# Gated scan: the second half of the causal convolution on VectorE instead of in TensorE's in-projection

## The reference, cut to what matters

```
xz = x @ W_in                          # 128 -> 512
xc, z = split(xz, 2)                   # 256 channels each
xt = causal depthwise conv of xc, 4 taps, own taps for each channel
u  = silu(xt)
dt_raw, B_raw = split(u @ W_x, 2)      # 16 + 16
dt = clip(softplus(dt_raw @ W_dt + b_dt), 1e-4, 1)
ub = u * (B_raw @ W_Bp)
h[t] = h[t-1] * (1 - dt[t]) + ub[t]
out = ((h + D_param * u) * silu(z)) @ W_out
```

## Time and profile before

| what | value |
|---|---|
| median of three runs | 3280.31 us |
| the profiled execution | 3282.22 us |
| its span | 3279.4 us |
| TensorE, busy share of the span | 79%, mean granted clock 0.91 |
| VectorE, busy share | 68% |
| ScalarE, busy share | 48% |
| GpSimd, busy share | 62% |

### The profile page before, as it was taken

The page is one execution under the profiler, slowest core; times in us unless marked ns, Lnnn a source line. Parts: engine busy times, 40 slices in busy tenths (PEclk is TensorE's granted clock), DMA queues, the critical chain, the costliest instruction groups (busy, mean ns, idle before and its releaser), DMA issues. The chain is left out here.

```text
span 3279.4 us, 43901 instructions
## 1 busy us (share of the span) xinstructions
PE 2580.4 (79%) x12400; PEld 1850.5 (56%) x12400; DVE 2222.7 (68%) x3998; ACT 1575.7 (48%) x2668; POOL 2018.0 (62%) x1643
## 2 busy tenths in 40 slices
PE   5799994996689999348996678788877875579782
PEld 4599993443579999327995233333332322559672
DVE  5656663786766666683332699999999998653333
ACT  4433333884533333333333667567577662443330
POOL 0377771232057776305772789999999784335776
PEclk9999997998599999569998899999999999589997
DMA  6111112100411111422332689889888886312333
GB/s 180 32 48 48 46 48 56 39 26 1 135 37 48 46 47 40 134 72 61 87 87 43 243 291 310 278 296 305 285 291 301 288 300 207 103 40 76 92 90 85
DMA packets 287326, 429.78 MB, mean 131 GB/s; under 512 B 59196, under 2 KB 196799, under 8 KB 287200
## 3 DMA queue, kind: packets, MB, share of 16 engines
q1 hardware_dynamic: 251744, 357.54, 33.1%
q0 software_dynamic: 35456, 70.86, 9.3%
HBM read 367.71 MB, written 62.39 MB: 131 GB/s over the span
## 5 line engine op out<-in xcount | busy, mean ns | idle before, releaser
L683 POOL DMA_INDIRECT m_rows<-rows_in,m_source x568 | 554.0, 975 | 588.6 <-SPq L580 222.2
L1593 PE MATMUL s_y_ps<-s_prod,ident 128*128 128x512 f32 x1024 | 522.0, 634 | 214.3 <-DVE s_prod L1880 214.3
L1558 POOL TENSOR_TENSOR s_dBu<-s_du,s_B_row 128x1024 f32<-128x1024 f32 x256 | 602.4, 2359 | 84.6 <-DVE s_dA L1873 71.1
L1873 DVE TENSOR_TENSOR_SCAN s_dA<-s_dA,s_dBu 128x1024 f32<-128x1024 f32 x256 | 585.6, 2287 | 44.3 <-POOL s_dBu L1558 44.3
L721 PE MATMUL m_A_ps<-m_rowsT,m_own 128*128 128x256 f32 x2272 | 569.0, 383 | 2.1 <-ACT m_rowsT L763 1.1
L737 PE MATMUL m_Y_ps<-m_own,m_hid 128*128 128x128 f32 x4544 | 556.1, 276 | 3.6 <-issue 3.6
L737 PEld LDWEIGHTS m_Y_ps<-m_own,m_hid 128*128 128x128 f32 x4544 | 531.4, 192 | 5.7 <-issue 5.6
L1593 PEld LDWEIGHTS s_y_ps<-s_prod,ident 128*128 128x128 f32 x1024 | 180.9, 195 | 523.3 <-DVE s_prod L1880 325.9
L773 ACT ACTIVATE m_act_a<-m_A_ps,m_own 128x256 f32<-128x256 f32 x568 | 238.5, 471 | 434.7 <-PE m_A_ps L721 318.9
L721 PEld LDWEIGHTS m_A_ps<-m_rowsT,m_own 128*128 128x128 f32 x2272 | 414.9, 193 | 48.8 <-ACT m_rowsT L763 1.9
L1694 ACT ACTIVATE s_dA<-s_delta,s_decay 128x1024 f32<-128x1024 f32 x256 | 286.0, 1118 | 311.0 <-DVE s_prod L1880 306.2
(11 more groups left out here) (241 smaller groups left out, 3543.9 us busy)
## 6 DMA issues: line engine op xcount, KB each, us to landing
s_B_row<-s_bc_rows SPq DMA_DIRECT2D x256, 512.0 KB, 5.7
s_C_row<-s_bc_rows SPq DMA_DIRECT2D x256, 512.0 KB, 6.0
rows_out<-m_y_sb SPq DMA_DIRECT2D x142, 128.0 KB
rows_in<-m_xs SPq DMA_DIRECT2D x64, 256.0 KB, 2.3
m_rows<-rows_in,m_source POOLq DMA_INDIRECT x568
s_got<-rows_by_token SPq DMA_DIRECT2D x16, 512.0 KB, 5.0
m_got<-rows_by_token SPq DMA_DIRECT2D x32, 256.0 KB, 3.9
rows_by_token<-m_y_sb,m_target POOLq DMA_INDIRECT x284
```

Source lines behind the costliest of these rows:

```text
L683: pool.indirect_dma_start(rows[:, b % AHEAD, r, :], None, c.rows_in, bass.IndirectOffsetOnAxis(source[:, 2 * b + r:2 * b + r + 1], 0)).the ...
L1558: nc.gpsimd.tensor_tensor(dBu[q % RING][:, :], du[s % 2][:, h, :], B_row[q % RING][:, :], ALU.mult).then_inc(dBu_ready, 1)
L1593: ins = nc.tensor.matmul(y_ps[:, at(cc, 512)], c.ident[:, :], prod[q % 2][:, at(cc, 512)], start=(n == 0), stop=(n == NS - 1))
L1873: nc.vector.tensor_tensor_scan(dA[q % 2][:, :], dA[q % 2][:, :], dBu[q % RING][:, :], 0.0, ALU.mult, ALU.add).then_inc(scanned, 1)
```

## The change

All of the first half's path is now taken for both halves. The four-tap matmuls, `w_conv`, `tap_rows`, its load and its multiplications go; so does `activated`. The banks of the four in-projections now stand together at the head of the pass.

```diff
-    ON_PE = (1,)
-    ON_DVE = tuple(m for m in range(HALVES) if m not in ON_PE)
-        w_conv = sb("w_conv", [D, CONV, INNER])
-        tap_rows = sb("tap_rows", [D, CONV, INNER])
-        N_DVE = len(ON_DVE) * HC
+        N_DVE = HALVES * HC
-                            (v + 1, (("in", range(N_DVE, HALVES * HC)), ("z", range(HALVES * HC)), ("low", range(HC)),
+                            (v + 1, (("z", range(HALVES * HC)), ("low", range(HC)),
-            load(tap_rows[:, :, :], w["taps"].rearrange("(a k) i -> a k i", a=1).to_broadcast([P, CONV, INNER]))
...
-                    if m in ON_PE:
-                        for tap in range(CONV):
-                            ins = nc.tensor.matmul(use.ps[:, :], w_conv[:, tap, at(m, P)],
-                                                   xnT[:, cc * 512 + tap:cc * 512 + tap + 512],
-                                                   start=(tap == 0), stop=(tap == CONV - 1))
-                    else:
-                        ins = nc.tensor.matmul(...)
+                    ins = nc.tensor.matmul(...)
...
                 if has(v + 1):
-                    project_in(v + 1, range(N_DVE, HALVES * HC))
                     project_z(v + 1)
...
-            def activated(t):
...
-                for i, m in enumerate(ON_DVE):
-                    act.wait_ge(conv_step, (t * len(ON_DVE) + i + 1) * (CONV - 1))
+                for i, m in enumerate(range(HALVES)):
+                    act.wait_ge(conv_step, (t * HALVES + i + 1) * (CONV - 1))
                     nc.scalar.activation(u[t % 2][:, m, :], conv[:, m, :], ACT.Silu).then_inc(u_ready, 1)
...
-                    activated(v + 1)
...
-            for tap in range(CONV):
-                nc.vector.tensor_tensor(w_conv[:, tap, :], w_in[:, 0:INNER], tap_rows[:, tap, :], ALU.mult).then_inc(conv_taps, 1)
...
             def convolve(t):
-                for i, m in enumerate(ON_DVE):
+                for i, m in enumerate(range(HALVES)):
```

More of the change, by code:

```diff
@@ L942, in gated_scan @@
         free = [sem(f"bank{i}_free") for i in range(BANKS)]
-        loaded, cleared, conv_taps, wide_scaled = sem("loaded"), sem("cleared"), sem("conv_taps"), sem("wide_scaled")
+        loaded, cleared, wide_scaled = sem("loaded"), sem("cleared"), sem("wide_scaled")
         rows_here, added, stat_done = sem("rows_here"), sem("added"), sem("stat_done")
@@ L980, in taken @@
                 eng.wait_ge(self.free, self.before + 1)
-        in_order = [(m, cc) for m in ON_DVE + ON_PE for cc in range(HC)]
-        LOADS = (8 + 2 * COPIES) * 16
+        in_order = [(m, cc) for m in range(HALVES) for cc in range(HC)]
+        LOADS = (7 + 2 * COPIES) * 16
         block = ctx.enter_context(nc.Block())
@@ L1043, in _ @@
             pe.wait_ge(cleared, 5)
-            pe.wait_ge(conv_taps, CONV)
             pe.wait_ge(wide_scaled, 2)
@@ L1064, in project_in @@
                     use.fill(pe)
-                    if m in ON_PE:
-                        for tap in range(CONV):
-                            ins = nc.tensor.matmul(use.ps[:, :], w_conv[:, tap, at(m, P)],
-                                                   xnT[:, cc * 512 + tap:cc * 512 + tap + 512],
-                                                   start=(tap == 0), stop=(tap == CONV - 1))
-                    else:
-                        ins = nc.tensor.matmul(use.ps[:, :], w_in[:, at(m, P)],
-                                               xnT[:, CONV - 1 + cc * 512:CONV - 1 + (cc + 1) * 512], start=True, stop=True)
+                    ins = nc.tensor.matmul(use.ps[:, :], w_in[:, at(m, P)],
+                                           xnT[:, CONV - 1 + cc * 512:CONV - 1 + (cc + 1) * 512], start=True, stop=True)
                     ins.then_inc(use.full, 1)
@@ L1150, in projected @@
                     use.read(act)
-                    wait(act, conv_step, t * len(ON_DVE) * (CONV - 1))
+                    wait(act, conv_step, t * HALVES * (CONV - 1))
                     nc.scalar.copy(xpad[:, m, CONV - 1 + cc * 512:CONV - 1 + (cc + 1) * 512], use.ps[:, :]).then_inc(xpad_ready, 1)
@@ L1258, in convolve @@
                             Use("in", t, k).taken(dve)
-                    done = (t * len(ON_DVE) + i) * (CONV - 1)
+                    done = (t * HALVES + i) * (CONV - 1)
                     for step in range(CONV - 1):
```

## The result

The changed kernel takes 3314.45 us, median of four runs (3313.76 to 3316.78), against 3280.42 for the kernel before beside it (3279.01 to 3281.13): a ratio of 1.0106, 95% interval [1.0088, 1.0123]. It is 34.0 us slower; 36.4 were forecast, and the range held it.

What follows compares the result with a forecast made beforehand. A loop through VectorE's convolve and statistics, GpSimd, ScalarE's normalisation and TensorE's wide projections bounds the pass. 26.2 without the clock + 9.0 clock + 1.2 in v = 6 = 36.4 us, so 3316.7 us; range 3303 to 3326.

Steps and rivals of the forecast that it cites:

- The loop through the statistics: Gated scan: a pass of 28.88 us loops through VectorE's convolve and statistics, GpSimd, ScalarE's normalisation and TensorE's wide projections.
- The added VectorE work: Three more convolve steps a sequence ahead of the statistics, 1285 ns each, lengthen each steady pass by 3.86 us.
- ScalarE's 2.2 us hidden: ScalarE's two more PSUM reads, 2.2 us a pass, are covered by its wait for GpSimd, which grows to about 2.2.
- The clock: TensorE's two longer pauses a pass lower its clock; slow matmuls after the second lengthen the loop, 9.0 us in all.
- The first fall: Clock fall in TensorE's low projection, hidden: it ends by 667.7 even if slow, ScalarE copies `xp` only from 668.5.
- seven shares of 0.9 to 1.35: Clock cost on the loop: 1.35 us in each of v = 0 to 5 and 0.9 in the first pass, 9.0 together.
- Three of four: Weight 3/4 on a 1.8 us slow spell: six of eight selective-scan pauses of 2.5 to 3.6 us were followed by slow matmuls.
- The case without falls in the clock: Rival: the clock holds through TensorE's longer pauses, so only 26.2 us are added, 3306.5 us; chance 0.20.
- v = 6 and the tail: Last pass, with no sequence left to normalise: 0.4 us from VectorE's work plus 1.2 from the slow low projection.
- The start: Layer's start: one load and its 0.43 us issue go from SyncE's queue, taken as -0.5 us.
- the bound of 1.7: Other bound for the layer's start: a free queue may give up to 1.7 us, the time of 512 KB.

Runs made afterwards that it cites:

- the fillers: Changed kernel with unused matmuls in one TensorE pause: ahead of the wide projections alone 3309.61 us, ahead of the low projection alone 3314.23 us.
- the filled kernel: Changed kernel with unused matmuls on TensorE in both pauses of a pass, ahead of the low and the wide projections: 3307.44 us, ratio 1.0086.

## Why the prediction was right, point by point

- **The loop through the statistics: right.** It is shown from two sides: 5.2 us off TensorE alone shorten no steady pass, and the statistics ahead of the convolution take back about 4 us of each, 2.3 by the order and 1.7 by the clock.
- **The added VectorE work: right, a little small.** L1236 ran 48 times at 1285 ns. But three more steps cost 4.05 us a pass, not 3 x 1.285 = 3.86. Each step waits for the one before it: within a half the starts stand 1.32 us apart, between the halves 1.42, which makes 1.32 + 1.32 + 1.42 = 4.06. Where there is no such wait, the next operation starts sooner: 1.20 us after the last step (666.49 - 665.29), and 1.17 us between the two `y` operations of the same type and shape. No run took the waits away, so this is a reading of the traces. The term was to be read from the distance of the starts, and not from the durations; that the whole of `convolve` measured 3.85 before, near 3 x 1.285, hid it.
- **ScalarE's 2.2 us hidden: right.** It waited 2.87 us for GpSimd (2.2 expected), as its z ended only 1.6 us later after `convolve` than before. They come out when VectorE's are taken away (30.8 us a pass).
- **The clock: right in mechanism, in place and in sum, wrong in how it is spread.** In v = 1 to 5 the first pause was 5.49 us and the second 2.3 to 3.8. The first fall is hidden, the second isn't; both are shown by the fillers and by the equal starts behind low projections of 5.20 and 6.67 us. Once the statistics are out of the loop the first fall shows: ScalarE then waits 0.6 to 0.9 us for the slow low projection. v = 1 to 5 paid 1.7, 1.7, 1.7, 1.4 and 3.0 us, v = -1 and 0 nothing; seven shares of 0.9 to 1.35 had been put in. The sum was 9.5, forecast 9.0. "Three of four" was counted in another layer; here the wide projections ran slow in five passes of seven, after pauses of 2.3 to 3.8 us, with none after 1.5 and 2.1. The case without falls in the clock (3306.5) is what the filled kernel approaches with 3307.4.
- **v = 6 and the tail: +0.1 instead of +1.6.** Up to the last scan the forecast held: the last sequence's L1242 began 29.30 us after the last convolve, where L1269 before had begun 27.85 after, +1.45. Then the last out-projection took 5.38 us instead of 6.75, because the clock rose sooner after it began; that gave 1.4 back. It has the same pause of 14.55 us ahead of it in both kernels. This is the clock's timing in one execution rather than the change: behind the same pause the same 32 matmuls took 5.59 and 5.74 us in variants of the kernel before, and 6.78 in the changed kernel with the load put back.
- **The start: -2.8 instead of -0.5, outside the bound of 1.7.** The forecast counted the load's own issue and not that the issue behind it had stalled for 2.14 us, which stood in the trace. By the run with the load put back, 1.0 us belongs to the load. The stall stands in five of five traces with the code of the kernel before and in none of seven with that of the changed one, so it very likely belongs to the change as well, by a cause that stays open.

The misses cancel in part, and that is luck: 2.3 at the start, 1.5 in the tail and 1.8 in the first two passes came out lower; the steady passes higher, by about 0.5 each for v = 1 to 3, 0.3 for v = 4 and 1.9 for v = 5. That is 5.6 us one way and 3.7 the other.

## What to carry to other kernels

The busiest engine need not be the bound: TensorE was busy 27.1 of 29.0 us, and 5.2 us less of it shortened no steady pass. Follow the releasers around the loop, and ask of each piece of work whether it stands ahead of or behind the operation that the loop goes through. Relief on TensorE has a price of its own when it opens pauses, and only the burst that nothing hides pays it. On an engine whose steps wait for each other, take a step's cost from start to start.

## What was not expected of the hardware

- Two pauses of equal length, 3.29 and 3.28 us, in neighbouring passes of one execution, were followed by eight matmuls of 5.37 and 3.67 us. A rule by the pause's length gives an average, not a pass.
- GpSimd's small L1019 took 2.01 us with VectorE's scans beside it, and 1.13 when the statistics came first and VectorE was convolving.
- The same DMA issue on SyncE, of 4 KB, took 2.14 us in the kernel before and 0.43 in the changed kernel with the same load ahead of it; the third issue of the layer took 1.43 to 2.14 us in all five traces with the code of the kernel before, whichever load it was.
